# Decoder layer on one core: expert numbers worked out and loaded by TensorE during its warming products, row places later, query halves cleared by GpSimd

## The chip, the cores and the metric

The kernel runs on one core of a Trainium2 chip. The metric is the device time in microseconds (us) of one execution; the median of three runs is given. The engines are TensorE (PE in the profile, its weight loads PEld, its sequencer PEldq or PEq), VectorE (DVE), ScalarE (ACT), GpSimd (POOL) and SyncE (SP), whose queue issues the DMAs.

## The reference

The input x has 4 batches of 256 tokens with 256 features. Three blocks follow one another, each a residual with a layer norm behind it: causal self-attention with 16 heads of 16 features; an expert block in which the token's id chooses one of four experts; and a routed feed-forward block in which the token's own logits choose one of four larger experts.

```python
x = _layernorm(x + _L0_attn_ref(x, q_proj, k_proj, v_proj, o_proj))
x = _layernorm(x + _L0_xattn_ref(x, itok, ctx, ctx, ctx))
x = _layernorm(x + _L0_ffn_ref(x, Wr, br, Wg, Wu, Wd))
...
expert_ids = jnp.minimum(tid // tokens_per_expert, E - 1)      # second block
...
top_w, top_idx = jax.lax.top_k(probs, 1)                       # third block
```

## The kernel before, in words

The program is written out by hand for each engine; an engine works through its own list in order, and semaphores tie the lists together. Products are made in float16 with each float32 operand split in a high part (ScalarE) and a low part (VectorE), so that a product becomes three matmuls (`three`, line 1281).

**First stage.** The tokens are eight tiles of 128, two to a batch. `qkv(tt)` (lines 1297 to 1316) projects a tile: six matmuls of 512 columns for query and key, six of 256 for the value. ScalarE copies the high parts out (`proj_hi`, lines 566 to 582), VectorE the low parts (`proj_lo`, line 928, its instructions on line 935), TensorE transposes them (`stack_T`, lines 1318 to 1329), and VectorE and ScalarE copy the transposes into QT and KT (`stacks`, lines 942 and 945; `q_odds`, line 593). Then `scores(b, g)` (lines 1331 to 1366) makes the scores of four heads for the row maxima, which VectorE takes (`maxima`, lines 956 and 961), and `scores_T(b, g)` (lines 1368 to 1389) makes the transposed scores for the exponentials. The maxima of batch 0 go by four small DMAs (line 385) into a row of QT before `scores_T(0, 0)` may start. In QT the rows of a head's other half must be zero; those of QT[0] are cleared by VectorE (lines 920 and 921, semaphore `const_z`), those of QT[1] and QT[2] by GpSimd (lines 468 to 471, `const_q2`).

**Sorting.** Six of the eight tiles are sorted by the expert of the second block. VectorE makes one-hot rows from the ids (lines 898 to 904); TensorE counts them with two small matmuls (`count`, line 1274, lines 1278 and 1279); VectorE copies the counts out (`counts`, lines 818 and 819), sums them (`running`, line 812), and works out which expert each of the nine sorted tiles belongs to (`slot_tiles`, lines 801 to 808, the last instruction writes `tile_i` and raises `tile_rdy`). `slots` (lines 824 to 832) works out the row of every token (`pos_i`, semaphore `pos_rdy`), which GpSimd needs for the scatter of the first block's rows. `pick` (lines 906 and 907) is a table for the two tiles that aren't sorted. TensorE later reads the nine expert numbers into registers (`expert_numbers`, lines 1461 to 1463, four of them ahead of `qkv(2 * TB)`, five behind `stack_T(3)`), since the second block addresses its weights by them.

**Start of TensorE.** Behind the two count matmuls stand thirty products whose result nobody reads, `keep_warm(WARM_START, before)` (line 1442, the matmul on line 1291), then `qkv(0)`.

**Order of the queues around the change.** VectorE: one-hot rows, pick, low parts of x for batch 0 (line 911), low parts of the projection weights (line 916), counts, clearing of QT[0], low parts for batch 1, expert numbers, row places, then `proj_lo(0)`. GpSimd: constants and masks (lines 425 to 464), clearing of QT[2] and QT[1], then the fill row (lines 473 and 474), for which SP waits with two large DMAs that fill the scratch for sorted rows. SP: inputs, those two fills, the maxima's rows, then the chunks of the feed-forward weights (line 374), the first of which waits for `x_lo` of all four batches.

## Time and profile before

| | us |
|---|---|
| median of 3 runs | 292.88 |
| lowest and highest run | 290.88, 294.34 |
| profiled execution, its own time | 293.57 |
| span of that execution in the profile | 291.8 |
| TensorE busy, share of the span | 234.3, 80% |
| VectorE busy | 191.7, 66% |
| ScalarE busy | 135.3, 46% |
| GpSimd busy | 66.1, 23% |

The profile covers the one profiled execution; its instructions start at 0 and end at 291.8 us, so 1.8 us of that execution's time lie outside the span. Averages over the span say little here, since the change touches only the first 45 us of it. A timeline row is one or several like instructions of an engine in a row, with its idle time before them and what ended it; "issue" means that nothing the profile shows was waited for. The chain that ended last is followed back from the last instruction and printed in order of time.

### The profile page before, as it was taken

How to read it: one execution, taken by the hardware profiler on the slowest of the kernel's cores; microseconds unless marked ns; L12 is line 12 of the kernel's file. 1: busy time of each engine (PE TensorE's matmuls, PEld its weight loads, DVE VectorE, ACT ScalarE, POOL GpSimd, SP SyncE). 2: the span in 40 equal slices, each digit the busy share in tenths (PEclk: the TensorE clock that was granted, in tenths of full speed). 3: DMA queues.
4: the chain of work that ended last, by engine and by line, in shares of the span. 5: the costliest groups of instructions: out<-in, count | busy, mean ns of one | idle time of the engine just before them, and what ended most of it. 6: DMA issues, size and time to landing. Idle time of an engine off the chain costs nothing.

```text
span 291.8 us, 7077 instructions
## 1 busy us (share of the span) xinstructions
PE 234.3 (80%) x2714; PEld 189.1 (65%) x2730; DVE 191.7 (66%) x425; ACT 135.3 (46%) x229; POOL 66.1 (23%) x128
## 2 busy tenths in 40 slices
PE   4568678988899897599997346898778999999970
PEld 4356355665676664367796222598768999999960
DVE  4887648786699685569988452789535555556550
ACT  4536355766694885256555151488131333333300
POOL 8500000100020444212122556000113212222222
PEclk9999779999999999789999558999999999999996
DMA  6999244142024444602409412340000000000000
GB/s 189 340 315 318 74 144 152 67 147 72 3 85 135 109 115 177 163 2 72 147 20 403 161 59 81 94 111 2 0 20 20 4 13 20 21 20 20 7 5 15
DMA packets 17424, 28.63 MB, mean 98 GB/s; under 512 B 2733, under 2 KB 12974, under 8 KB 17392
## 3 DMA queue, kind: packets, MB, share of 16 engines
q1 hardware_dynamic: 16048, 25.28, 27.5%
q0 software_dynamic: 1344, 2.90, 2.8%
q8 instruction: 23, 0.38, 0.6%
q14 instruction: 9, 0.07, 0.1%
HBM read 19.43 MB, written 9.50 MB: 99 GB/s over the span
## 4 chain that ended last, share of the span: by engine, by line
PE 56%; DVE 21%; issue 9%; ACT 5%; POOL 4%; DMA 3%; SPq 1%; POOLq 0%; DVEq 0%; ACTq 0%
PE ps L1285 9%; PE ps L1678 7%; PE ps L1679 7%; PE ps L1680 7%; PE ps L1695 3%; PE ps L1697 3%; PE ps L1696 3%; DVE wf_lo L795 3%; PE ps L1362 3%; POOL sorted L519 2%; DVE arena L961 2%; PE ps L1614 2%; DMA ring<-wqkvT 2%; PE ps L1358 2%; ACT wf_hi L559 1%
## 5 line engine op out<-in xcount | busy, mean ns | idle before, releaser
L1678 PE MATMUL ps<-arena,wf_hi 128*128 128x128 f16 x352 | 60.2, 219 | 0.3 <-DVE arena L1197 0.3
L1679 PE MATMUL ps<-arena,wf_hi 128*128 128x128 f16 x352 | 60.3, 218 | 0.0
L1680 PE MATMUL ps<-arena,wf_lo 128*128 128x128 f16 x352 | 60.2, 217 | 0.0
L1679 PEld LDWEIGHTS ps<-arena,wf_hi 128*128 x352 | 34.3, 98 | 0.2
L1678 PEld LDWEIGHTS ps<-arena,wf_hi 128*128 x352 | 33.7, 96 | 0.9 <-issue 0.8
L1680 PEld LDWEIGHTS ps<-arena,wf_lo 128*128 x352 | 33.9, 96 | 0.0
L1695 PE MATMUL ps<-wf_hi,arena 128*128 x88 | 24.0, 273 | 5.9 <-DVE arena L1222 3.4
L795 DVE SCALAR_TENSOR_TENSOR wf_lo<-ring,wf_hi 128x1024 f16<-128x1024 f32 x17 | 20.6, 1219 | 11.0 <-ACT wf_hi L559 5.9
L751 ACT ACTIVATE arena<-ps 128x512 f32<-128x512 f32 x22 | 13.1, 594 | 29.7 <-PE ps L1680 29.7
L1697 PE MATMUL ps<-wf_hi,arena 128*128 x88 | 24.0, 273 | 0.0
L1696 PE MATMUL ps<-wf_lo,arena 128*128 x88 | 24.0, 273 | 0.0
L1285 PE MATMUL ps<-xT_hi,arena 128*128 (+1 forms) x88 | 21.5, 309 | 1.7 <-DVE arena L1137 1.1
L1206 DVE SCALAR_TENSOR_TENSOR arena<-ps,arena 128x512 f32<-128x512 f32 x22 | 15.2, 691 | 10.3 <-PE ps L1680 9.5
L758 ACT ACTIVATE arena<-arena 128x512 f16<-128x512 f32 x22 | 13.8, 629 | 16.6 <-DVE arena L1206 16.6
L1285 PE MATMUL ps<-arena,xT_hi 128*128 128x512 f16 (+1 forms) x64 | 16.5, 348 | 6.3 <-DVE xT_lo L911 2.6
L1213 DVE TENSOR_TENSOR arena<-arena 128x512 f16<-128x512 f32 x22 | 15.2, 691 | 8.8 <-ACT arena L758 8.8
L961 DVE TENSOR_REDUCE arena<-ps 128x4 f16<-128x1024 f32 x16 | 19.6, 1222 | 0.2
L536 POOL TENSOR_SCALAR veps<-mv 128x1 f32<-128x1 f32 x11 | 2.5, 226 | 71.1 <-DVE mv L1228 71.1
L559 ACT ACTIVATE wf_hi<-ring 128x1024 f16<-128x1024 f32 x17 | 17.7, 1054 | 0.1
L610 ACT ACTIVATE arena<-ps 128x1024 f32<-128x1024 f32 x16 | 16.6, 1036 | 1.1 <-PE ps L1385 0.7
L956 DVE TENSOR_REDUCE arena<-ps 128x4 f16<-128x512 f32 x16 | 11.0, 690 | 8.3 <-PE ps L1362 8.1
L1385 PE MATMUL ps<-arena 128*128 128x128 f16 x144 | 12.7, 227 | 3.3 <-issue 2.8
(223 smaller groups left out, 562.8 us busy)
## 6 DMA issues: line engine op xcount, KB each, us to landing
ring<-Wf SPq DMA_DIRECT2D x17, 512.0 KB, 3.7
sorted<-fill SPq DMA_DIRECT2D x1, 4515.0 KB, 20.8
arena<-Wf SPq DMA_DIRECT2D x7, 512.0 KB, 8.1
arena<-sorted SPq DMA_DIRECT2D x20, 129.0 KB, 2.3
sorted<-fill SPq DMA_DIRECT2D x1, 1161.0 KB, 6.3
ring<-xT SPq DMA_DIRECT2D x4, 256.0 KB, 5.1
X<-x_tok SPq DMA_DIRECT2D x1, 1024.0 KB, 7.8
ring<-ctxT SPq DMA_DIRECT2D x2, 512.0 KB, 3.6
```

Source lines behind the costliest of these rows:

```text
L559: a.activation(chunk_dst(ORDER[n], True), src, ACT.Copy, scale=W_SCALE).then_inc(c_hi, 1)
L610: a.activation(Pf[n % 2][:, 1:3], ps[:, 4:6, :], ACT.Exp, scale=DK ** -0.5).then_inc(exped, 1)
L795: v.scalar_tensor_tensor(out=chunk_dst(ORDER[n], False), in0=staged(n)[0], scalar=W_SCALE, in1=chunk_dst(ORDER[n], True), op0=ALU.mult, op ...
L961: v.tensor_reduce(dst[:, 1], ps[:, 1:3, :].rearrange("p c (a k) -> p a c k", a=G), AX.XY, ALU.max, negate=True).then_inc(maxed, 1)
L1206: v.scalar_tensor_tensor(out=hh[:, half * 512:(half + 1) * 512], in0=ps[:, 2 * half + 1, :], scalar=inv, in1=sg[:, half * 512:(half + 1) * ...
L1285: last = t.matmul(dst, xs(k), ws(k), start=(k == 0 and m == 0), stop=(k == nk - 1 and m == 2))
L1678: t.matmul(dst, hi, a_hi[p][:, k], start=k == 0, stop=False)
L1679: t.matmul(dst, hi, a_lo[p][:, k], start=False, stop=False)
L1680: last = t.matmul(dst, lo, a_hi[p][:, k], start=False, stop=k == NK - 1)
L1695: t.matmul(ps[:, 7, 0:D], hs[:, c], hi, start=c == 0, stop=False)
L1696: t.matmul(ps[:, 7, 0:D], hs[:, c], lo, start=False, stop=False)
L1697: last = t.matmul(ps[:, 7, 0:D], ls[:, c], hi, start=False, stop=c == NF - 1)
```

## The change

Five edits, all in the first stage:

1. VectorE works out the expert numbers (`counts`, `running`, `slot_tiles`) directly behind the one-hot rows, ahead of the low parts of x and of the weights.
2. VectorE makes `pick` and the row places (`slots`) later, behind `stacks(3)` and ahead of the low parts of batch 3 (`x_low(3)`) and of `maxima(1, 0)`.
3. The two clears of QT[0] go from VectorE to GpSimd, ahead of those of QT[2] and QT[1]; GpSimd waits for `const_z` between them.
4. TensorE makes 15 warming products in place of 30, waits for `tile_rdy`, and then loads the nine expert numbers, each followed by three more warming products (WARM_START // 10), 42 in all. The loads at the two later places are gone.
5. TensorE waits for `const_z` ahead of `scores(0, 0)`.

```diff
--- before.py
+++ after.py
@@ -465,6 +465,9 @@
                             base=0, pattern=[[0, G], [1, P]], channel_multiplier=-1).then_inc(const_m, 1)
 
             pool.wait_ge(const_m, 2)
+            link(g.memset(QT[0][SLOT:P, 0::2, :].bitcast(F32), 0.0))
+            g.memset(QT[0][0:SLOT, 1::2, :].bitcast(F32), 0.0).then_inc(const_z, 1)
+            pool.wait_ge(const_z, 1)
             link(g.memset(QT[2][SLOT:P, 0::2, :].bitcast(F32), 0.0))
             g.memset(QT[2][0:SLOT, 1::2, :].bitcast(F32), 0.0).then_inc(const_q2, 1)
             link(g.memset(QT[1][SLOT:P, 0::2, :].bitcast(F32), 0.0))
@@ -903,8 +906,11 @@
             link(ins)
             v.tensor_tensor(oh[:, 0:NA, :].rearrange("p i e -> p e i"), ge[:, 0:E, 0:NA], ge[:, 1:E + 1, 0:NA],
                             ALU.subtract).then_inc(oh_rdy, 1)
-            link(v.tensor_tensor(pick[:, :, :], ge[:, 0:E, NA:NT], ge[:, 1:E + 1, NA:NT], ALU.subtract))
-            v.tensor_scalar(pick[:, :, :], pick[:, :, :], 1 / W_SCALE, None, ALU.mult).then_inc(pick_rdy, 1)
+            counts()
+            dve.wait_ge(cnt_sb, 1)
+            running()
+            slot_tiles(0, NA)
+
             def x_low(b):
                 dve.wait_ge(x_hi, b + 1)
                 t = slice(b * S, (b + 1) * S)
@@ -915,15 +921,7 @@
                 dve.wait_ge(w_hi, k + 1)
                 v.scalar_tensor_tensor(out=wqkv_lo[:, k], in0=wqkv_st[:, k], scalar=W_SCALE, in1=wqkv_hi[:, k],
                                        op0=ALU.mult, op1=ALU.subtract).then_inc(w_lo, 1)
-            counts()
-
-            v.memset(QT[0][SLOT:P, 0::2, :].bitcast(F32), 0.0)
-            v.memset(QT[0][0:SLOT, 1::2, :].bitcast(F32), 0.0).then_inc(const_z, 1)
             x_low(1)
-            dve.wait_ge(cnt_sb, 1)
-            running()
-            slot_tiles(0, NA)
-            slots()
 
             def proj_lo(tt):
                 j = tt % 2
@@ -1029,6 +1027,9 @@
             stacks(2)
             proj_lo(2 * TB)
             stacks(3)
+            link(v.tensor_tensor(pick[:, :, :], ge[:, 0:E, NA:NT], ge[:, 1:E + 1, NA:NT], ALU.subtract))
+            v.tensor_scalar(pick[:, :, :], pick[:, :, :], 1 / W_SCALE, None, ALU.mult).then_inc(pick_rdy, 1)
+            slots()
             x_low(3)
             maxima(1, 0)
             dve.wait_ge(w_hi, NK + 1)
@@ -1439,7 +1440,12 @@
                                  lambda k: wo_hi[:, k], lambda k: wo_lo[:, k], NK)
                     last.then_inc(wo_rdy, 1)
 
-            keep_warm(WARM_START, before[:, :])
+            keep_warm(WARM_START // 2, before[:, :])
+            pe.wait_ge(tile_rdy, 1)
+            experts = []
+            for k in range(NSA):
+                experts.append(pe.value_load(tile_i[0:1, 0, k:k + 1], min_val=0, max_val=E - 1))
+                keep_warm(WARM_START // 10, before[:, :])
             pe.wait_ge(x_lo, 1)
             pe.wait_ge(w_lo, NK)
             qkv(0)
@@ -1448,6 +1454,7 @@
             stack_T(0)
             stack_T(1)
             pe.wait_ge(const_m, 1)
+            pe.wait_ge(const_z, 1)
             scores(0, 0)
             pe.wait_ge(x_lo, 2)
             qkv(2)
@@ -1456,19 +1463,10 @@
             scores(0, 2)
             stack_T(2)
             scores(0, 3)
-            experts = []
-
-            def expert_numbers(n):
-                for k in range(len(experts), n):
-                    experts.append(pe.value_load(tile_i[0:1, 0, k:k + 1], min_val=0, max_val=E - 1))
-
-            pe.wait_ge(tile_rdy, 1)
-            expert_numbers(4)
             pe.wait_ge(x_lo, 3)
             pe.wait_ge(maxed, 2 * NG - 1)
             qkv(2 * TB)
             stack_T(3)
-            expert_numbers(NSA)
             for step in range(STEPS):
                 b, g = divmod(step, NG)
                 if step == 0:
@@ -1545,7 +1543,6 @@
                                        identF[:, :])
                 last.then_inc(bhT, 1)
 
-            expert_numbers(NSA)
             for s in range(NS + LOGIT_LAG):
                 if s < NS:
                     k = sorted_of(s)
```

TensorE at the start, before: the warming products (L1291) and the first matmuls of `qkv(0)` (L1285).

```order
L1291 MATMUL ps<-before,ones 128x128 x30
L1285 MATMUL ps<-arena,xT_hi 128x512 [waits w_lo,x_lo]
L1285 MATMUL ps<-arena,xT_hi 128x512
L1285 MATMUL ps<-arena,xT_lo 128x512
L1285 MATMUL ps<-arena,xT_hi 128x512 x2
```

TensorE at the start, changed kernel, where one load is a TENSOR_LOAD with two more sequencer instructions (ISA) behind it:

```order
L1292 MATMUL ps<-before,ones 128x128 x15
L1447 TENSOR_LOAD tile_i [waits tile_rdy]
L1447 ISA x2
L1292 MATMUL ps<-before,ones 128x128 x3
L1447 TENSOR_LOAD tile_i
L1447 ISA x2
L1292 MATMUL ps<-before,ones 128x128 x3
L1447 TENSOR_LOAD tile_i
L1447 ISA x2
L1292 MATMUL ps<-before,ones 128x128 x3
L1447 TENSOR_LOAD tile_i
```

The pattern of one load and three products comes nine times, and the matmuls of `qkv(0)` stand behind the last. 

TensorE at the end of `scores(0, 3)` (L1358 and L1362), before, up to `qkv(2 * TB)`:

```order
L1358 MATMUL ps<-maskS,identB 128x512
L1362 MATMUL ps<-arena 128x128 x4
L1463 TENSOR_LOAD tile_i [waits tile_rdy]
L1463 ISA x2
L1463 TENSOR_LOAD tile_i
L1463 ISA x2
L1463 TENSOR_LOAD tile_i
L1463 ISA x2
L1463 TENSOR_LOAD tile_i
L1463 ISA x2
L1285 MATMUL ps<-arena,xT_hi 128x512 [waits maxed,x_lo]
L1285 MATMUL ps<-arena,xT_hi 128x512
```

The same place in the changed kernel, where line numbers are one higher:

```order
L1359 MATMUL ps<-maskS,identB 128x512
L1363 MATMUL ps<-arena 128x128 x4
L1286 MATMUL ps<-arena,xT_hi 128x512 [waits maxed,x_lo]
L1286 MATMUL ps<-arena,xT_hi 128x512
L1286 MATMUL ps<-arena,xT_lo 128x512
```

Nothing stands between the two any more; the five loads behind `stack_T(3)` are gone in the same way.

VectorE behind the one-hot rows, before (L911 and L916 are the low parts of x and of the weights):

```order
L904 TENSOR_TENSOR oh<-ge 128x4x6 [waits link_v]
L906 TENSOR_TENSOR pick<-ge 128x8
L907 TENSOR_SCALAR pick<-pick 128x8 [waits link_v]
L911 TENSOR_TENSOR xT_lo<-ring,xT_hi 128x2x256 [waits x_hi]
L916 SCALAR_TENSOR_TENSOR arena<-ring,arena 128x768 [waits w_hi] x2
L818 COPY cum<-ps 128x24 [waits cnt_rdy]
L819 COPY cnt<-ps 128x4x6
L920 MEMSET arena 64x8x128
L921 MEMSET arena 64x8x128
L911 TENSOR_TENSOR xT_lo<-ring,xT_hi 128x2x256 [waits x_hi]
L812 SCALAR_TENSOR_TENSOR run<-reset,cnt 128x44 [waits cnt_sb]
L801 TENSOR_TENSOR over<-run,steps 128x32 [waits link_v]
```

VectorE at the same place in the changed kernel:

```order
L907 TENSOR_TENSOR oh<-ge 128x4x6 [waits link_v]
L821 COPY cum<-ps 128x24 [waits cnt_rdy]
L822 COPY cnt<-ps 128x4x6
L815 SCALAR_TENSOR_TENSOR run<-reset,cnt 128x44 [waits cnt_sb]
L804 TENSOR_TENSOR over<-run,steps 128x32 [waits link_v]
L806 TENSOR_REDUCE nt_e<-over 128x4 [waits link_v]
L807 SCALAR_TENSOR_TENSOR end_e<-reset,nt_e 128x4 [waits link_v]
L808 TENSOR_TENSOR tile_ge<-tiles,end_e 128x33 [waits link_v]
L810 TENSOR_REDUCE tile_e<-tile_ge 128x11 [waits link_v]
L811 CAST tile_i<-tile_e 128x11 [waits link_v]
L917 TENSOR_TENSOR xT_lo<-ring,xT_hi 128x2x256 [waits x_hi]
L922 SCALAR_TENSOR_TENSOR arena<-ring,arena 128x768 [waits w_hi] x2
```

The nine instructions from the counts to `tile_i` moved ahead of the low parts, and the two clears are gone. VectorE behind `stacks(3)`, before:

```order
L942 COPY arena<-ps 128x8x128 [waits kT_rdy]
L945 COPY arena<-ps 64x8x128 [waits qT_rdy]
L911 TENSOR_TENSOR xT_lo<-ring,xT_hi 128x2x256 [waits x_hi]
L956 TENSOR_REDUCE arena<-ps 128x4 [waits s_rdy]
L961 TENSOR_REDUCE arena<-ps 128x4 [waits s_rdy]
```

VectorE behind `stacks(3)` in the changed kernel:

```order
L940 COPY arena<-ps 128x8x128 [waits kT_rdy]
L943 COPY arena<-ps 64x8x128 [waits qT_rdy]
L1030 TENSOR_TENSOR pick<-ge 128x8
L1031 TENSOR_SCALAR pick<-pick 128x8 [waits link_v]
L827 TENSOR_TENSOR base_e<-end_e,nt_e 128x4
L828 TENSOR_TENSOR run<-run,cnt 128x4x6 [waits link_v]
L829 SCALAR_TENSOR_TENSOR run<-base_e,run 128x4x6 [waits link_v]
L831 TENSOR_TENSOR where<-cum,run 128x24 [waits link_v]
L833 TENSOR_TENSOR where<-where,oh 128x24 [waits link_v]
L834 TENSOR_REDUCE pos<-where 128x6 [waits link_v]
L835 CAST pos_i<-pos 128x6 [waits link_v]
L917 TENSOR_TENSOR xT_lo<-ring,xT_hi 128x2x256 [waits x_hi]
```

Nine instructions for `pick` and `slots` now stand between the copies of `stacks(3)` and the low parts of batch 3, with the maxima of batch 1 behind those.

## Rows read from the trace of the kernel before

**Rows 1.** Chain that ended last, 0 to 60 us: start, duration, what.

```profile
16.16 0.69 DVE arena L942
...
30.52 0.50 issue
31.02 2.73 PE ps L1285 x6
...
36.24 0.60 DVE arena L945
...
42.00 1.23 DVE arena L961
```

**Rows 2.** TensorE timeline: start, duration, instruction, idle before it and releaser.

```profile
3.65 3.36 PE L1291 MATMUL ps<-before,ones 128*128 128x128 f16 x30
9.05 0.59 PE L1285 MATMUL ps<-arena,xT_hi 128*128 128x512 f16 x2 [2.03 <-DVE arena L916]
...
15.51 0.62 PE L1323 MATMUL ps<-identH,arena 128*128 128x128 f16 x8 [2.40 <-DVE arena L935]
...
19.11 0.61 PE L1362 MATMUL ps<-arena 128*128 128x128 f16 x8 [1.65 <-DVE arena L945]
...
31.02 1.01 PE L1285 MATMUL ps<-arena,xT_hi 128*128 128x512 f16 x2 [2.60 <-DVE xT_lo L911]
...
38.47 1.06 PE L1385 MATMUL ps<-arena 128*128 128x128 f16 x8 [2.79 <-issue]
```

**Rows 3.** Line 1463, sequencer of TensorE: count, minimum/median/maximum ns, first and last start.

```profile
L1463 PEldq TENSOR_LOAD <-tile_i x9: 294/303/978, 27.6 to 37.1; - x9
```

**Rows 4.** The same loads between 27 and 31 us only.

```profile
L1463 PEldq TENSOR_LOAD <-tile_i x4: 294/306/978, 27.6 to 30.3; - x4
```

**Rows 5.** VectorE timeline, 0 to 60 us.

```profile
4.84 1.08 DVE L911 TENSOR_TENSOR xT_lo<-ring,xT_hi 128x512 f16<-128x512 f32 x1 [0.74 <-ACT xT_hi L563]
...
8.91 0.17 DVE L819 COPY cnt<-ps 128x24 f32<-128x24 f32 x1
...
10.51 0.91 DVE L921 MEMSET arena<- 64x1024 f32 x1 [0.25 <-issue]
11.35 0.62 DVE L911 TENSOR_TENSOR xT_lo<-ring,xT_hi 128x512 f16<-128x512 f32 x1
11.89 0.23 DVE L812 TENSOR_TENSOR_SCAN run<-reset,cnt 128x44 f32<-128x44 f32 x1
...
13.26 0.17 DVE L808 CAST tile_i<-tile_e 128x11 int32<-128x11 f32 x1
...
14.62 0.17 DVE L832 CAST pos_i<-pos 128x6 int32<-128x6 f32 x1
...
41.27 0.69 DVE L956 TENSOR_REDUCE arena<-ps 128x4 f16<-128x512 f32 x1 [3.84 <-PE ps L1362]
```

**Rows 6.** GpSimd timeline, 0 to 60 us.

```profile
4.74 0.64 POOL L458 TENSOR_SCALAR_AFFINE_SELECT maskS<-maskS 128x512 bf16<-128x512 bf16 x1
...
6.86 0.95 POOL L468 MEMSET wf_hi<- 64x1024 f32 x1
```

**Rows 7.** Windows: PE, PEld, DVE, ACT, POOL busy, granted clock, DMA share, GB/s.

```profile
160.70:174.30 13.60, 5.04 (x20) 3.53 (x19) 6.58 (x37) 4.06 (x8) 8.00 (x10) 0.50 0.29 111
31.02:34.40 3.38, 3.38 (x11) 1.49 (x12) 1.34 (x3) 0.63 (x2) 0.00 (x0) 0.50 0.07 15
38.10:41.20 3.10, 2.73 (x20) 2.28 (x22) 0.00 (x0) 1.38 (x2) 0.00 (x0) 0.50 0.89 305
```

**Rows 8.** DMA issues by the SP queue, 0 to 60 us.

```profile
29.96 2.71 SPq L385 DMA_DIRECT2D arena<-arena  x4
37.46 12.78 SPq L374 DMA_DIRECT2D ring<-Wf  x5
```

**Rows 9.** Landing of the chunk DMAs of line 374, 36 to 60 us.

```profile
DMA to landing us min/median/max: 3.4/3.8/4.7
```

**Rows 10.** ScalarE timeline, first weight chunk.

```profile
46.63 1.06 ACT L559 ACTIVATE wf_hi<-ring 128x1024 f16<-128x1024 f32 x1
```

## Prediction

> **What bounds the kernel now.** I read the chain that ended last first, then the timelines of TensorE, VectorE and GpSimd for the first 45 us, then the sequencer's register loads, and last the windows with the granted clock. The reader is to see three things.
>
> First, TensorE is not short of work but of inputs. It stands idle for 2.03 us before `qkv(0)`, 2.40 us before the first transposes and 1.65 us before the first scores [rows 2], each time for VectorE. The chain runs over VectorE's copies from 16.16 us on [rows 1]. In the second gap VectorE is busy with two clears (0.91 us each, 0.25 us between), batch 1's low parts, the expert numbers (start of L812 at 11.89, end of L808 at 13.43) and the row places (until 14.79) [rows 5].
>
> Second, the nine expert numbers stand in TensorE's way twice. The loads are made by its sequencer, in order: four start between 27.6 and 30.3 us [rows 4], the last of nine at 37.1 us [rows 3]. The first took 0.978 us, the others about 0.30, but they follow each other at (30.3 - 27.6 - 0.68) / 3 = 0.67 us, since two further sequencer instructions belong to each. The low parts were there at 30.52 us, and `qkv(4)` started at 31.02 [rows 1]: 0.5 us is the loads'. VectorE's last copy ended at 36.84 us (36.24 + 0.60) [rows 1], and the transposed scores are first seen at 38.47 us, after 2.79 us of idleness put down to "issue" [rows 2]: some 1.3 us is the loads', the rest the first mask product, whose record is missing.
>
> Third, the clock. Behind the gaps of 2.60 and 2.79 us the granted clock is 0.50, the 1.2 GHz level: from 31.02 to 34.40 and from 38.10 to 41.20 us [rows 7]. Eight products of 128 columns take 1.06 us at 38.47 against 0.61 at 19.11 [rows 2]. Half of these 6.5 us is lost: 1.7 and 1.55 us.
>
> **The change, part by part.** All times are of the profiled execution.
>
> *Expert numbers first.* The count products are issued just ahead of 3.65 us [rows 2], so the counts can be copied at about 3.95 us. Two copies take 0.3 us (one is 0.17 [rows 5]) and the chain to `tile_i` 1.54 us (11.89 to 13.43): 5.8 us at the earliest. That chain ran with GpSimd nearly idle. Now it stands beside GpSimd's masks and clears (L458 from 4.74, L468 from 6.86 to 7.81 us [rows 6]), and beside them the subtraction on line 911 took 1.08 us in place of 0.62 [rows 5, 6]. If two of the chain's instructions are held by the masks, and its last waits for the end of L468, it ends at 8.0. I take 7.0, with 5.8 and 8.0 as ends.
>
> The Trainium skill ("SBUF — State Buffer", section "Who interferes with whom") says that VectorE and GpSimd share one port pair as an exclusive lock, which VectorE wants with two SBUF inputs against a reading GpSimd instruction, or in a two-port mode. By that rule the chain goes to the late end, 8.0 us, and the sum below becomes 1.0 us larger; were there no lock, 1.2 us smaller. The 1.08 us row agrees with the rule.
>
> *Loads at the start.* TensorE's sequencer waits there for `tile_rdy`. Queued behind it are the products between the loads and all of `qkv(0)`. The first load costs 0.98 + 0.37 = 1.35 us, eight more 0.67 each: 6.7 us, so that `qkv(0)` starts at 7.0 + 6.7 + 0.2 = 13.9 us instead of 9.05: +4.85. Nothing hides this: VectorE's work behind the chain is pushed back by 7.0 - 4.84 = 2.2 us at most [rows 5], so the low parts are there by 9.05 + 2.2 = 11.2 us. The 27 products between the loads are issued ahead of their running and cost the sequencer next to nothing; the upper end, if it waited for each three (3 x 0.112 us, from 3.36 / 30 [rows 2]), is 3.0 us more. Below, a first load without the 0.68 us of surplus gives 0.7 less.
>
> *Clock at `qkv(0)`.* Before, 30 unbroken products ran at the 1.2 GHz level (0.112 us apart), and `qkv(0)` met the 2.4 GHz level: two products of 512 columns in 0.59 us, against 1.01 at 31.02 [rows 2]. Now 15 products end near 5.3 us, a pause follows, then three at a time (0.34 us) in every 0.67. Each rise I see comes behind unbroken products, as those of 31.02 to 34.40 us; from 160.7 to 174.3 us, with products in 5.04 of 13.6 us, the clock stayed at 0.50 [rows 7]. So I let `qkv(0)` run at the low level and rise after some 3.3 us, as it did behind 31.02: +1.65. Ends: nothing, and +3.9 if `qkv(1)` is slow too.
>
> *What VectorE gives back.* Both projections took 4.05 us (9.05 to 13.10: 15.51 less 2.40); they now end at 13.9 + 4.05 + 1.65 = 19.6. VectorE has no clears, numbers or places left to do. The query and key part of `qkv(1)` (two thirds of its columns) is done at 18.95. At `qkv(4)` that part ended at 33.75 (31.02 + 2.73) and VectorE's two copies began at 36.84 - 1.2 = 35.65 [rows 1]: 1.9 us for the copies of ScalarE and the low parts. So `stacks(0)` starts at 20.85 instead of 16.16 [rows 1]: +4.7. So of 6.5 us, 1.8 comes back.
>
> *Loads gone at 28 us.* The gap before `qkv(4)` shrinks from 2.60 to 2.1 us, the 0.5 us is gained (+4.2), and I take the clock to stay at 1.00: the query and key part takes 1.35 in place of 2.73 us [rows 1]. VectorE's last copy ends at 36.84 + 4.2 - 1.35 = 39.7. Ends: all 1.35 lost if the clock falls.
>
> *Loads gone at 35 to 37 us.* The transposed scores follow the copy by 0.25 us, at 39.95 instead of about 38.1: +1.85. Their low stretch of 3.1 us is gone, 1.55 back: TensorE is +0.3 at 41.2 us.
>
> *`pick` and `slots` late.* Nine instructions, 1.4 us for `slots` (13.43 to 14.79 [rows 5]) and 0.35 for `pick` (an estimate, two more like them), from 39.7 to 41.5 us, then `x_low(3)` 0.62 (L911 [rows 5]): `maxima(1, 0)` starts at 42.15 instead of 41.27 [rows 5]: +0.9. The 3.84 us in which VectorE was idle there [rows 5] hid them before; now they outlast the scores. The second maximum was on the chain at 42.00 [rows 1] and starts at 42.75: +0.75, which the chain carries on. `pos_rdy` and `pick_rdy` are wanted by the scatters and the dense tiles, tens of us later.
>
> *The rest.* GpSimd's clears of QT[0] end at 8.8 us, long before the scores. They push the fill row, and so the fill DMAs, 2.0 us later. These were done at 31 us (DMA share 0.07 from 31.02 on [rows 7]), now at 33; the four DMAs of the maxima (issued 29.96 to 32.67 [rows 8]) now start at 34.6 and are in by 39. The first weight chunks wait for `x_low(3)`: 42.2 instead of 37.46 [rows 8], landing 3.8 us later [rows 9], at 46.0; ScalarE wants the first at 46.63 [rows 10], now 47.4. Hidden, by 1.4 us.
>
> **Sum.** +4.85 + 1.65 - 1.8 - 0.5 - 1.35 - 1.0 (loads at 37 us) - 1.55 + 0.5 (VectorE over TensorE) = +0.8 us. The profiled execution took 293.57, so 294.4; it stood 0.69 over the median of 292.88, so the forecast for the median is 293.7 us. A change within 1% is about what a measurement of this kernel can't tell from none.
>
> **The rivals.**
> - *A: loads cheap.* If the loads ran beside the warming products or at 0.3 us, `qkv(0)` would start at about 9.5, the copy of line 945 end at 36.84 + 0.45 - 2.3 (VectorE's clears and places) - 0.5 - 1.35 = 33.1, and `maxima(1, 0)` start at 35.6: 5.6 us less, 287.3. For it: the gaps at 13 to 15 us are real. Against: 0.67 us apart [rows 4] while little else ran.
> - *B: the clock is up at once.* 1.65 us less than forecast: 292.1. For it: the 15 products in front. Against: the stretch 160.7 to 174.3.
> - *C, slower: the low level lasts.* The broken products keep the clock at 0.50 until the scores: 3.9 instead of 1.65 us for both projections and 0.8 us more for the last sixteen transposes, 296.7 us. It decides if the clock is still 0.50 when `stack_T(1)` runs, near 21 us. For it: no rise in the trace comes behind broken products. Against: `qkv(0)` and `qkv(1)` are unbroken for over 5 us.
> - *D: the change doesn't do what it says*, in that the loads' 6.7 us don't leave the path but move to where TensorE has nothing else. This is the forecast itself.
>
> **How the numbers follow.** Forecast 0.52, C 0.22, A 0.13, B 0.13. Low end of the forecast's terms: -1.2 (chain) - 0.7 (first load) gives 291.8, with B 290.2. High end: +1.0 (chain) and a fall of the clock at `qkv(4)` +1.35 gives 296.1; C with the late chain 297.7. Range 290.2 to 297.2. Faster by over 1% (under 289.95): A and a little of B, 0.15. Slower by over 1% (over 295.8): most of C and a tail of the forecast, 0.20. Within 1%: 0.65.
>
> **What would show it.** Right: nine loads from 7 to 13.5 us, `qkv(0)` starting at 13 to 14.5 us at clock 0.50, no idle time on TensorE between `qkv(1)` and `stack_T(0)`, first scores near 23.5 us, `qkv(4)` behind the low parts within 0.1 us at clock 1.00, `maxima(1, 0)` at 42 behind x's low parts, and from there on all rows shifted alike. Wrong: `qkv(0)` before 11 us (A), a clock of 1.00 at its start (B) or of 0.50 at 21 us (C), a wait for the maxima's rows before the transposed scores, or a clock that falls elsewhere after 110 us.

## The result, and the profile after

The changed kernel took 296.86 us, median of four runs (295.34 to 299.03), against 292.76 for the kernel before beside it (290.88 to 294.34): ratio 1.0167, interval 1.0124 to 1.0211. A ratio leaves out disturbed (slow) executions, so it need not match the two medians beside it. The kernel is slower; the forecast was 293.7 us and no change worth speaking of. The time lies inside the stated range, but the kernel did change, by more than 1%.

| | before | after |
|---|---|---|
| median of the runs | 292.76 us | 296.86 us |
| profiled execution, its span | 293.57, 291.8 us | 296.75, 294.6 us |
| mean granted clock | 0.939 | 0.933 |

TensorE's timeline of the changed kernel, where it answers to [rows 2]:

```profile
3.65 1.76 PE L1292 MATMUL ps<-before,ones 128*128 128x128 f16 x15
6.99 0.50 PE L1292 MATMUL ps<-before,ones 128*128 128x128 f16 x3 [1.58 <-DVE tile_i L811]
...
12.36 0.50 PE L1292 MATMUL ps<-before,ones 128*128 128x128 f16 x3 [0.20 <-issue]
12.65 1.06 PE L1286 MATMUL ps<-arena,xT_hi 128*128 128x512 f16 x2
...
16.30 0.59 PE L1286 MATMUL ps<-arena,xT_hi 128*128 128x512 f16 x2
...
18.25 0.61 PE L1324 MATMUL ps<-identH,arena 128*128 128x128 f16 x8
...
22.52 0.61 PE L1363 MATMUL ps<-arena 128*128 128x128 f16 x8 [1.73 <-DVE arena L943]
...
33.98 0.60 PE L1286 MATMUL ps<-arena,xT_hi 128*128 128x512 f16 x2 [2.14 <-DVE xT_lo L917]
...
39.12 0.61 PE L1386 MATMUL ps<-arena 128*128 128x128 f16 x8 [2.13 <-DVE arena L943]
```

`qkv(0)` starts at 12.65 us in place of 9.05. Its products run at the 1.2 GHz level (two of 512 columns in 1.06 us), those of `qkv(1)` at 16.30 at 2.4 GHz (0.59). The first scores come at 22.52 us, 3.4 us late. But the transposed scores, at 39.12, are only 0.65 us behind the 38.47 of [rows 2], and eight of their products take 0.61 us where they took 1.06.

The nine loads by line, which answer to [rows 3, 4]:

```profile
L1447 PEldq TENSOR_LOAD <-tile_i x9: 294/304/493, 6.1 to 11.7; - x9
```

They again follow each other at (11.7 - 6.1 - 0.2) / 8 = 0.67 us. VectorE's timeline, against [rows 5]:

```profile
3.84 0.18 DVE L821 COPY cum<-ps 128x24 f32<-128x24 f32 x1 [0.39 <-PE ps L1280]
...
4.14 0.25 DVE L815 TENSOR_TENSOR_SCAN run<-reset,cnt 128x44 f32<-128x44 f32 x1
...
4.87 0.50 DVE L807 TENSOR_TENSOR_SCAN end_e<-reset,nt_e 128x4 f32<-128x4 f32 x1
...
5.86 0.17 DVE L811 CAST tile_i<-tile_e 128x11 int32<-128x11 f32 x1
5.94 0.79 DVE L917 TENSOR_TENSOR xT_lo<-ring,xT_hi 128x512 f16<-128x512 f32 x1
...
37.87 0.67 DVE L943 COPY arena<-ps 64x1024 f16<-64x1024 f16 x1
38.47 0.15 DVE L1030 TENSOR_TENSOR pick<-ge 128x8 f32<-128x8 f32 x1
...
40.10 0.69 DVE L917 TENSOR_TENSOR xT_lo<-ring,xT_hi 128x512 f16<-128x512 f32 x1
40.70 0.69 DVE L954 TENSOR_REDUCE arena<-ps 128x4 f16<-128x512 f32 x1
41.31 1.23 DVE L959 TENSOR_REDUCE arena<-ps 128x4 f16<-128x1024 f32 x1
```

The numbers were there at 6.03 us. The second maximum stands at 41.31 against 42.00 on the chain before [rows 1]: in these two executions the changed kernel is 0.69 us *ahead* there, and stays so up to 118 us (118.16 and 117.48 us for the same instruction of VectorE). What it loses, it loses later, where TensorE's clock is low. The windows of the changed kernel:

```profile
12.70:16.00 3.30, 3.30 (x12) 1.47 (x10) 0.00 (x0) 0.55 (x2) 1.15 (x6) 1.00 0.39 129
31.00:34.40 3.40, 1.26 (x12) 0.75 (x12) 3.19 (x6) 0.62 (x1) 0.00 (x0) 1.00 0.66 182
38.10:41.20 3.10, 2.08 (x28) 1.85 (x30) 2.86 (x12) 2.19 (x3) 0.00 (x0) 1.00 0.00 0
118.60:128.60 10.00, 7.88 (x36) 5.72 (x37) 3.85 (x10) 2.80 (x8) 0.04 (x1) 0.50 0.27 76
163.00:179.80 16.80, 8.35 (x26) 4.26 (x27) 6.86 (x38) 5.31 (x8) 11.05 (x14) 0.50 0.20 74
183.40:186.70 3.30, 3.30 (x9) 1.36 (x10) 2.16 (x2) 0.17 (x1) 0.00 (x0) 0.50 0.30 83
207.30:210.60 3.30, 3.30 (x18) 2.30 (x17) 0.21 (x1) 0.00 (x0) 0.00 (x0) 0.50 0.00 0
```

and of the kernel before, for the same stretches of its work:

```profile
119.80:126.50 6.70, 5.40 (x24) 3.76 (x25) 3.22 (x9) 2.31 (x6) 0.00 (x0) 0.50 0.36 100
160.80:177.70 16.90, 8.27 (x28) 4.67 (x27) 8.17 (x45) 5.70 (x9) 9.98 (x13) 0.50 0.25 95
183.40:186.70 3.30, 2.20 (x14) 0.90 (x12) 1.87 (x3) 1.32 (x3) 0.00 (x0) 1.00 0.36 91
207.30:210.60 3.30, 3.30 (x51) 3.16 (x49) 1.16 (x4) 0.49 (x1) 0.44 (x2) 1.00 0.00 0
```

A warning for the reading of the clock column: the window at 12.70 says 1.00, and the products in it take 1.06 us for two of 512 columns, the time of the low level. In all these profiles the column reads 1.00 up to the first fall, whatever the products take; there the durations have to be read (here they turn short between 16.06 and 16.19 us).

Two explanations of 4 us were open: something in the first stage that this pair of profiles hides, or low stretches in the last two blocks that the change brings about.

### The profile page after: what moved, and what is told of

Same layout as the page of the kernel before. It is cut to its first block, busy times and chain, and to the rows that moved or that the text cites. A ratio compares the mean times of both kernels' runs of the same rounds, so it can differ in the third digit from the quotient of the medians.

```text
span 294.6 us, 7101 instructions
## 1 busy us (share of the span) xinstructions
PE 240.1 (81%) x2726; PEld 190.9 (65%) x2742; DVE 189.6 (64%) x423; ACT 135.4 (46%) x229; POOL 68.7 (23%) x130
## 4 chain that ended last, share of the span: by engine, by line
PE 59%; DVE 20%; issue 9%; ACT 5%; POOL 3%; DMA 2%; POOLq 0%; DVEq 0%; ACTq 0%
PE ps L1286 11%; PE ps L1675 7%; PE ps L1676 7%; PE ps L1677 7%; PE ps L1692 4%; PE ps L1693 3%; PE ps L1694 3%; PE ps L1292 3%; PE ps L1363 2%; DVE arena L959 2%; DVE wf_lo L798 2%; PE ps L1611 2%; POOL sorted L522 2%; ACT wf_hi L562 1%; DVE arena L954 1%
## 5 line engine op out<-in xcount | busy, mean ns | idle before, releaser
L1692 PE MATMUL ps<-wf_hi,arena 128*128 x88 | 24.7, 281 | 5.9 <-DVE arena L1223 3.4
L1693 PE MATMUL ps<-wf_lo,arena 128*128 x88 | 24.8, 282 | 0.0
L1694 PE MATMUL ps<-wf_hi,arena 128*128 x88 | 24.8, 281 | 0.0
L1286 PE MATMUL ps<-xT_hi,arena 128*128 (+1 forms) x88 | 22.5, 318 | 2.0 <-DVE arena L1138 1.4
L543 POOL DMA_INDIRECT out<-arena,out_i x11 | 12.0, 1091 | 13.9 <-DVE arena L1235 13.9
L933 DVE SCALAR_TENSOR_TENSOR arena<-ps,arena 128x256 f16<-128x256 f32 x16 | 6.0, 419 | 13.6 <-ACT arena L582 13.6
```

What stands on the lines that cost most here:

```text
L1286: last = t.matmul(dst, xs(k), ws(k), start=(k == 0 and m == 0), stop=(k == nk - 1 and m == 2))
L1692: t.matmul(ps[:, 7, 0:D], hs[:, c], hi, start=c == 0, stop=False)
L1693: t.matmul(ps[:, 7, 0:D], hs[:, c], lo, start=False, stop=False)
L1694: last = t.matmul(ps[:, 7, 0:D], ls[:, c], hi, start=False, stop=c == NF - 1)
```

## The experiments

**The moment at which the products begin.** The first idea was that the low stretches behind 118 us depend on when TensorE's products begin. `late_warm` and `later_warm` are the kernel before with a wait in front of the warming products and nothing else moved:

```diff
+            pe.wait_ge(const_m, 1)          # late_warm
             keep_warm(WARM_START, before[:, :])

+            pe.wait_ge(const_m, 2)          # later_warm
-            keep_warm(WARM_START, before[:, :])
+            keep_warm(2 * WARM_START // 3, before[:, :])
```

`warm_whole` is the changed kernel with all 30 products ahead of the loads; `vector_only` has VectorE's and GpSimd's part of the change, with TensorE's products and loads as before.

```diff
-            keep_warm(WARM_START // 2, before[:, :])      # warm_whole, from the changed kernel
+            keep_warm(WARM_START, before[:, :])
```

> The kernel before, with one wait more: the thirty warming products start behind GpSimd's first mask (about 5.4 us) instead of at 3.65 us, and end by about 8.9 us, so that the first projection still starts near 9.05 us at the 2.4 GHz level. Nothing else changes. Theory 1 (when the clock first rises decides at which later pauses of TensorE it falls): the first 100 us are as before within 0.3 us, the rise comes about 1.8 us later than at 7.1 us, and the falls after 110 us lie elsewhere and last longer or shorter; the time moves by 1.5 us or more, either way, all of it behind 110 us. Theory 2 (the loss lies in the late fill, the late row places or the moved expert numbers): same as before within 0.5 us, about 292.8.

> The kernel before, with the warming products (20 instead of 30) starting behind GpSimd's second mask at about 6.85 us. The first projection starts near 9.05 us still at the low level and loses about 0.6 us until the rise near 10.3 us. Theory 1: the moments at which the clock may change lie again nearly where they lay before, so the later falls are those of before, and the time is 0.3 to 1.0 us over before, 293.1 to 293.8; the first kernel of this call moves more than this one though its start is disturbed less. Theory 2: 0.6 us over before for the same reason, and the first kernel at nothing.

> The changed kernel with 30 instead of 15 products ahead of the loads, so that they run unbroken from 3.65 to 7.0 us, while the sequencer already makes the first load. Theory 1: the clock rises near 7.1 us as before; it may fall again during the three-product groups and rise during the first projection, but its changes stay where the kernel before has them, so the falls after 110 us are those of before, and with the first stage 0.6 us or more ahead the time is 291 to 293.5 us. Theory 2: nothing changes against the changed kernel, 296 to 297 us, since the loads end at 12.4 us all the same.

> The changed kernel with TensorE's part taken back: thirty unbroken warming products at 3.65 us, the loads at their two old places, four and five. VectorE's and GpSimd's parts are those of the change. Theory 1: the first scores come near 17 us instead of 19.1, the second projection group and the transposed scores 1.5 to 2 us earlier, less what the row places take back on VectorE (1.8 us), the clock rises at 7.1 us as before: 291 to 293 us. Theory 2 (the late fill or the row places cost the time): the 4 us stay, 296 to 297.

| | median (range) of its runs, us | before on the same chip | ratio, interval |
|---|---|---|---|
| late_warm | 294.02 (291.15 to 295.91) | 294.14 | 0.9993, 0.9958 to 1.0029 |
| later_warm | 294.53 (290.20 to 296.24) | 294.14 | 0.9897, 0.9826 to 0.9968 |
| warm_whole | 298.02 (295.22 to 302.08) | 294.14 | 1.0110, 1.0070 to 1.0150 |
| vector_only | 297.11 (294.77 to 300.71) | 294.14 | 1.0112, 1.0068 to 1.0157 |

`later_warm` has the lower ratio and the higher median, so it says nothing firm. The products of `late_warm` begin 1.8 us later (5.43 for 3.65 us) and its ratio has no room for the 1.5 us that theory 1 wanted, so the idea falls. `warm_whole` has twice the products in front and still first rises to the high level at 16.1 us, as the changed kernel does. `vector_only` is slow without any of TensorE's part. So VectorE's and GpSimd's part alone brings 3.0 us in the whole kernel, most of the loss. And the runs of the one kernel before went from 291.05 to 297.27 us here: a single profile is one draw from a spread wider than the effect.

**Where the loss is: the program cut.** To get the spread down I cut the program behind attention. The cut kernels leave out the second and third blocks (the expert block and the routed feed-forward block), and write X1, the rows that the attention block left, instead. All kernels named `stage_` are cut so.

```diff
             for m in range(n - RING, n):            # SP, then `return` on every engine
+                sp.wait_ge(*staged(m)[1:])
+            sp.wait_ge(res1, NT)
+            sp.wait_ge(x1_rdy, NA)
+            sp.dma_start(out.rearrange("(n p) d -> p n d", p=P), X1[:, :, 0:D]).then_inc(in_late[0], 16)
```

> The kernel before, cut off behind the attention stage (about 118 us): no second and third block; the first six token tiles after the first norm and the last two before it are written out as the result. It is the yardstick for the next two: about 118 us and one transfer of 1 MB, 124 to 128 us. Its executions spread with the clock's changes in the first 45 us, by up to 3 us.

> The changed kernel with the same cut. Theory A (the 4 us are lost in the first stage, in most executions, and the profiled ones happen to be good for the changed kernel and bad for the one before): its median is 3 to 4 us over that of the kernel before with the same cut. Theory B (the first stage is as the profiles show it, 0.7 us ahead, and the loss lies behind the attention, where the clock falls more often): its median is 0.7 us under to 0.5 us over.

> VectorE's and GpSimd's parts of the change alone, with the loads at their old places and 30 warming products, with the same cut. Theory A: 3 us over the kernel before with this cut, as its full version was. Theory B: within 1 us of it.

`stage_before` took 123.12 us (122.70 to 124.75), `stage_after` 125.81 (123.49 to 126.03), `stage_vector` 125.36 (123.82 to 126.94), six executions each on one chip. So by the medians 2.7 us are lost in the first stage, where the pair of full profiles had shown 0.69 us of gain: theory A, a little under its 3 to 4 us. That leaves 4.1 - 2.7 = 1.4 us of the whole kernels' loss that the cut kernels don't show. It may lie behind attention, where the changed kernel's profile has low stretches that the other lacks (183.40 and 207.30 us), or in the spread between sets of runs: the kernel before had medians of 292.49 to 294.19 us on the chips used here. Which of the two isn't shown.

The cut kernels below ran on four chips. The kernel before's medians beside them were 292.49 us (with `stage_before`), 293.84 (`stage_slots` to `clears`), 293.62 (`stage_loads` to `held`) and 294.19 (`stage_four` to `stage_held`), so a difference of under about 1 us between cut kernels of different sets isn't firm.

The rows where TensorE had waited, `stage_before` first:

```profile
9.12 1.01 PE L1297 MATMUL ps<-arena,xT_hi 128*128 128x512 f16 x2 [2.11 <-DVE arena L926]
...
19.19 0.61 PE L1374 MATMUL ps<-arena 128*128 128x128 f16 x8 [1.65 <-DVE arena L955]
31.13 0.59 PE L1297 MATMUL ps<-arena,xT_hi 128*128 128x512 f16 x2 [2.64 <-DVE xT_lo L921]
36.95 1.06 PE L1397 MATMUL ps<-arena 128*128 128x128 f16 x8 [2.81 <-issue]
43.07 0.62 PE L1335 MATMUL ps<-identH,arena 128*128 128x128 f16 x8 [0.32 <-DVE arena L966]
```

and `stage_after`:

```profile
22.12 1.06 PE L1375 MATMUL ps<-arena 128*128 128x128 f16 x8 [1.89 <-DVE arena L953]
35.07 0.72 PE L1298 MATMUL ps<-arena,xT_hi 128*128 128x512 f16 x2 [2.14 <-DVE xT_lo L927]
41.29 0.61 PE L1398 MATMUL ps<-arena 128*128 128x128 f16 x8 [1.52 <-ACT arena L605]
45.96 0.62 PE L1336 MATMUL ps<-identH,arena 128*128 128x128 f16 x8 [0.32 <-DVE arena L964]
```

with its two low windows:

```profile
21.80:25.10 3.30, 2.98 (x16) 1.94 (x18) 1.72 (x2) 0.00 (x0) 0.00 (x0) 0.50 1.10 235
35.50:38.80 3.30, 3.30 (x14) 1.75 (x13) 1.52 (x4) 1.08 (x2) 0.00 (x0) 0.50 0.05 8
```

Against [rows 2], this execution of the old order runs `qkv(4)` at the high level (0.59 for 1.01) and reaches the transposed scores at 36.95 in place of 38.47; this one of the new order has a low stretch from its first scores on and another inside `qkv(4)`, and reaches them at 41.29. A later row, the transposes behind the first maximum of batch 1, stands behind both places. The two full profiles, before first, have it at

```profile
44.48 0.62 PE L1323 MATMUL ps<-identH,arena 128*128 128x128 f16 x8 [0.32 <-DVE arena L956]
```

```profile
43.79 0.62 PE L1324 MATMUL ps<-identH,arena 128*128 128x128 f16 x8 [0.32 <-DVE arena L954]
```

The profile before was a slow draw in its first stage (44.48 for 43.07, 1.41 us), the profile after a quick one (43.79 for 45.96, 2.17 us): -0.69 + 1.41 + 2.17 = +2.89 us, which is how far apart the two cut profiles are.

**VectorE's edits one by one.** Three kernels, each `stage_before` with one of them:

```diff
+            link(v.tensor_tensor(pick...)); slots()     # shortened; stage_slots: only here, behind stacks(3)
             x_low(3)
             maxima(1, 0)

+            counts(); dve.wait_ge(cnt_sb, 1); running(); slot_tiles(0, NA)   # stage_numbers: only here
             x_low(0)

-            v.memset(QT[0]...)                          # stage_clears: by GpSimd behind const_m 2
```

`clears` is the third in the whole kernel.

> First stage alone, cut as stage_before was (second and third blocks left out), with one part of the change: pick and the row places moved behind stacks(3), in front of x_low(3) and maxima(1, 0). Theory L (the late row places are what costs): they stood at 13.41 to 14.85 us in front of proj_lo(0), and now hold maxima(1, 0) back by 1.6 us of VectorE's time, so the median is 1 to 1.6 us above stage_before's 123.1 (124.1 to 124.7). Theory F (it is when TensorE stands idle and then runs at the low level that costs, and the places are worth nothing by themselves): proj_lo(0) is 1.4 us earlier, scores(0, 0) too, and what is given back at the start pays for what is lost at 38 us: 122.3 to 123.6.

> First stage alone, same cut, with one part of the change: counts, running counts and tile numbers on VectorE ahead of x_low(0); row places, pick, the clears of QT[0] and TensorE's loads stay where they were. Theory L: x_low(0) and so qkv(0) start about 1.1 us late, but VectorE has the same time less to do before proj_lo(0), so nothing is left of it: 122.6 to 123.8. Theory F: qkv(0) starts later after the warming products, TensorE is idle between 7 and 10 us for longer, and qkv(0) falls to the low level in most executions, as in stage_vector's profile (9.75 to 13.16 us): 124.3 to 125.6, low level within 9.7 to 14 us in the profile.

> First stage alone, same cut, with one part of the change: QT[0] cleared by GpSimd instead of VectorE. VectorE has 2.0 us less between 9.4 and 11.4 us. Both theories: proj_lo(0) starts 1.5 to 2.1 us earlier, scores(0, 0) as well, unless x_low(1) waits for its rows. Theory L: the gain reaches the end, 121.2 to 122.4. Theory F: the gain is taken back where TensorE waits for scores, x_low(2) and maxima anyway: 122.3 to 123.5.

> The whole kernel with that one part (QT[0] cleared by GpSimd, all else as before). Theory L: 1 to 2 us faster than before on the same chip, ratio 0.993 to 0.997. Theory F: ratio 0.998 to 1.002, and the profile shows the start ahead by 1.5 us or more up to about 30 us and not behind it.

They took 123.38 us (122.73 to 125.84), 123.28 (123.02 to 124.67) and 123.50 (122.42 to 124.66): none differs from 123.12 by anything firm. `stage_numbers`' profile has the low level from 10.20 to 13.50 us, as theory F wanted, and took 123.09 us, so there it cost nothing. Both theories' larger figures fall: the late row places cost nothing alone and the moved clears give nothing alone. In `stage_slots`' profile the first maximum waits for its scores long after row places and `x_low(3)` are done:

```profile
36.77 0.17 DVE L842 CAST pos_i<-pos 128x6 int32<-128x6 f32 x1
36.85 0.68 DVE L919 TENSOR_TENSOR xT_lo<-ring,xT_hi 128x512 f16<-128x512 f32 x1
...
39.37 0.69 DVE L963 TENSOR_REDUCE arena<-ps 128x4 f16<-128x512 f32 x1 [1.83 <-PE ps L1374]
```

`clears`, the whole kernel, took 295.69 us (293.58 to 298.99) against 293.84, ratio 1.0085 (1.0038 to 1.0132). That is slower by more than its interval, which neither theory had, and the cut kernel shows only 0.4 us of it. I can't say from what. In its one profile, one of its longer executions (298.15 us), the clock is also low behind attention from 208 to 212 and from 222 to 225.5 us (windows of 0.57 and 0.51, where the kernel before has 1.00); that this is the rule is not shown.

**TensorE's part, a pair, and a short warming.** `stage_loads` adds to `stage_numbers` what the change does on TensorE; `stage_pair` has early numbers and late row places; `stage_half` is `stage_before` with 15 products.

```diff
-            keep_warm(WARM_START, before[:, :])           # stage_loads, from stage_numbers
+            keep_warm(WARM_START // 2, before[:, :])
+            pe.wait_ge(tile_rdy, 1)
+            experts = []
+            for k in range(NSA):
+                experts.append(pe.value_load(tile_i[0:1, 0, k:k + 1], min_val=0, max_val=E - 1))
+                keep_warm(WARM_START // 10, before[:, :])

-            keep_warm(WARM_START, before[:, :])           # stage_half, from stage_before
+            keep_warm(WARM_START // 2, before[:, :])
```

> First stage alone, same cut: stage_numbers plus TensorE's part of the change (15 products, then the nine loads with groups of three products, ahead of qkv(0)); row places, pick and the clears of QT[0] as before. Theory R (TensorE's part is what costs: broken products and loads keep the clock from rising before qkv(0), so qkv(0) and qkv(1) run at the low level, longer in some executions than in others): median 125.2 to 126.0, as stage_after's 125.8, the first rise in the profile at 14.5 us or later. Theory S (it needs clears and row places as well, since each part alone was worth nothing): 123.2 to 124.3.

> First stage alone, same cut: numbers early and row places late together, clears of QT[0] still on VectorE, TensorE as before; stage_vector without the moved clears. Theory R: the VectorE part costs by where the low level happens to lie, not by one of its edits, so 123.2 to 124.3 and a wide range. Theory S: early numbers and late row places together are stage_vector's loss, 124.8 to 125.6.

> First stage alone, same cut: the kernel before with 15 warming products in place of 30 and nothing else, so that TensorE stands idle from about 5.4 to 9.05 us. Theory R: the clock does not rise before qkv(0), which runs at the low level; rise at 12 us or later, median 124.5 to 126. Theory S: qkv(0) at the low level hides behind VectorE's row places and clears, which stand in front of proj_lo(0) here, so 123.0 to 123.8.

`stage_loads` took 125.99 us (124.13 to 126.41), 2.7 above `stage_numbers`, from which it differs on TensorE alone: theory R's size. `stage_half` took 123.97 (122.74 to 124.94), 0.85 above `stage_before` and between the two theories' ranges: three executions at 122.7 to 123.3, three at 124.6 to 124.9. Its `qkv(0)` started in time, at 9.18 us, and at the low level. There VectorE's clears and row places stand behind the projections and hide most of that: `stage_before`, whose `qkv(0)` also ran low in its profile (1.01), has its first scores at 19.19 us, against 19.11 for a `qkv(0)` at the high level [rows 2]. In `stage_loads` they don't hide it, since VectorE is done with them at 13.5 us and the transposes follow `qkv(1)` at once, at 17.76: the two projections take 5.11 us there for 4.05. So the low level is worth some 1 us of `stage_loads`' 2.7, by this one profile, and not all. `stage_pair` took 124.25 (121.40 to 125.58), inside R's range, three executions at 121.4 to 123.2 and three at 125.3 to 125.6.

**Place of the loads, or clock.** Two edits to `stage_loads` that tell these apart: four loads in front and five behind `stack_T(3)`; and all nine in front without the products between them.

```diff
-            for k in range(NSA):                 # stage_four; the other five behind stack_T(3)
+            for k in range(4):

-                keep_warm(WARM_START // 10, before[:, :])     # stage_no_groups
```

> First stage alone, same cut: stage_loads with only the first four loads (and their groups of products) ahead of qkv(0); the other five behind stack_T(3), where they were before. Theory P (the nine loads cost by where they stand: qkv(0) starts at 12.65 us in stage_loads' profile and at 9.05 in stage_numbers'): four loads end by 9.0 us, so qkv(0) starts at 9.1 to 9.4, and the median falls from stage_loads' 126.0 to 123.3 to 124.4. Theory C (it is the clock, which the broken products keep from rising before qkv(0)): the products are as broken as before, qkv(0) at the low level, 125.0 to 126.0.

> First stage alone, same cut: stage_loads without the groups of three products between the loads, so that TensorE multiplies nothing from 5.4 to about 12.6 us. Theory P: the groups hide behind the loads, which come 0.67 us apart with or without them; qkv(0) at 12.4 to 12.7, median 125.5 to 126.3, as stage_loads' 126.0. Theory C: the clock rises later still, and the median is above 126.5.

`stage_four` took 123.76 us (121.70 to 125.21), `stage_no_groups` 125.54 (123.82 to 125.84): both medians are theory P's. In `stage_four` the products were as broken as before and `qkv(0)` ran low, but it started at 9.26 us and not at 12.65, the first scores came at 19.61 and not at 22.14, and the median is 2.2 us lower. Three of its executions lie at 124.8 to 125.2 all the same, so its median stands between two groups. `stage_no_groups` is not above 126.5, as C wanted, with the first rise at 18.2 us against 15.1 in `stage_loads`. That doesn't show that the clock is free: its profile lacks the low stretch of `stage_loads` at 21.80 to 25.10 us, and the low level lasted about as long in both. Its row:

```profile
12.26 1.01 PE L1297 MATMUL ps<-arena,xT_hi 128*128 128x512 f16 x2 [6.86 <-DVE xT_lo L926]
```

against `stage_numbers`:

```profile
9.05 0.59 PE L1297 MATMUL ps<-arena,xT_hi 128*128 128x512 f16 x2 [2.12 <-DVE arena L931]
```

The start of `qkv(0)` moves by the loads' own time, with products between them or without (0.39 us less). Over all cut kernels: with nine loads in front 13 of 18 executions took over 125 us, and the quickest of each kernel 123.49 to 124.13; with none in front and at most one of VectorE's edits (`stage_before`, `stage_slots`, `stage_numbers`, `stage_clears`, `stage_half`), 2 of 30, and the quickest 122.42 to 123.02. So the medians' 2.7 us hold two things: the quick executions are some 1 us slower, and far more of the executions are long ones.

**What the two low stretches were worth.** `held` is the whole kernel before with products between its loads, in the places where TensorE had stood idle ahead of `qkv(4)` and of the transposed scores; `stage_held` is the same, cut.

```diff
+HOLD = 2
             for k in range(len(experts), n):
                 experts.append(pe.value_load(tile_i[0:1, 0, k:k + 1], min_val=0, max_val=E - 1))
+                for _ in range(HOLD if bank is not None else 0):
+                    t.matmul(ps[:, bank, :], identB[:, :], maskS[:, :, :].rearrange("p a k -> p (a k)"),
+                             start=True, stop=True)
-            expert_numbers(4)
+            expert_numbers(4, bank=7)
             stack_T(3)
+            pe.wait_ge(kT_done, 3)
-            expert_numbers(NSA)
+            expert_numbers(NSA, bank=3)
```

> The whole kernel before, all its parts, with two products of 128x512 behind each of the nine loads of expert numbers, in bank 7 for the first four (at 28 us) and bank 3 for the others (at 35 us). Theory R and every theory in which idle TensorE ahead of qkv(2 * TB) and of the transposed scores brings the low level at 31.0 to 34.4 and 37.8 to 41.2 us: neither stretch is at the low level in the profile, and the time is 0.5 to 2.5 us below before's on the same chip (ratio 0.991 to 0.998). If the stretches at the low level only come later: ratio 0.999 to 1.003.

> First stage alone, same cut: held, cut. If the stretches at the low level around 31 and 38 us are what an ordinary execution of the kernel before has, taking them away gives 2 to 2.9 us: 120.2 to 121.2. If its profiled execution was one with more of them than most, less: 121.5 to 122.7 (whole kernel: held's median was 1.15 us below that of before).

`held` took 292.47 us (290.11 to 294.94) against 293.62, ratio 0.9935 (0.9896 to 0.9974). It is faster than the kernel before, and so than the changed one. `stage_held` took 122.09 (121.87 to 122.77), 1.0 below `stage_before` (on another chip), and its five executions lie closer together than those of any other cut kernel. Its windows:

```profile
10.10:13.40 3.30, 3.30 (x12) 1.64 (x11) 2.88 (x9) 1.47 (x3) 1.30 (x6) 0.50 1.07 353
28.00:31.40 3.40, 2.81 (x17) 0.92 (x15) 3.23 (x7) 0.45 (x1) 0.00 (x0) 1.00 0.94 243
31.40:34.80 3.40, 3.40 (x33) 2.29 (x31) 1.89 (x6) 1.63 (x4) 0.00 (x0) 1.00 0.09 18
34.80:38.20 3.40, 3.19 (x23) 1.32 (x22) 1.85 (x4) 1.80 (x3) 0.00 (x0) 1.00 0.15 24
```

From 28 to 38 us TensorE is busy in 9.4 of 10.2 us, and the level is high. Neither stretch of [rows 7] is there, and by the medians that is worth 1.0 us, not the 2.9 which the one profile put on them. The 1.0 is net: `qkv(4)` starts at 31.49 us behind the added products and at 31.13 in `stage_before`. One reason why it isn't more stands in the profiles of the five cut kernels with the loads at their old places and at most one of VectorE's edits: four have one low stretch between 30 and 42 us (`stage_half` and `stage_numbers` at `qkv(4)`, `stage_before` and `stage_slots` behind it), and only `stage_clears` has both, as [rows 7] do.

## Why the prediction was wrong

**Right:**
- *Loads at the start.* 13.9 us was forecast for `qkv(0)`, it was 12.65. The step of 0.67 us for a load held to the hundredth. The difference, 1.25 us, is the chain (ready at 6.03 us, 7.0 taken, 5.8 the early end) and the first load's surplus, 0.2 us and not 0.68.
- *The chain and the port.* The Trainium skill ("SBUF — State Buffer", section "Who interferes with whom") led to the late end, 8.0 us. The chain's seven instructions took from 4.14 to 6.03, 1.89 us against 1.54 before; one scan with two inputs took 0.50 us for 0.17 beside GpSimd's mask, which agrees with the rule. But what contention there was cost 0.35 us, far from the late end.
- *Clock at `qkv(0)`.* Low, and up at 16.1 us, some 3.4 us on. The two projections took 5.6 us (12.65 to 18.25) for 4.05: +1.55, with +1.65 forecast. But that the kernel before has the high level there was also one draw: `stage_before` and `held` start `qkv(0)` at the low level behind the same 30 products (1.01 us for two).
- *What VectorE gives back.* Transposes straight behind `qkv(1)` (18.25 us), `stacks(0)` at 19.58; first scores 3.4 us late, with a start 3.6 us late and 1.55 us lost to the clock: 1.7 given back, 1.8 forecast.
- *`pick` and `slots` late.* They occupied VectorE from 38.47 to 40.19 us, as long as I thought. I charged 0.75 us; it was nothing, since the first maximum at 40.70 came as its scores ended.
- *No wait for the maxima's rows, chunks hidden.* Neither shows in the trace.

**The step that failed** is the clock behind `qkv(1)`: "I take the clock to stay at 1.00" at `qkv(4)`, -1.35 us, with "their low stretch ... is gone", -1.55 us, and no term at all for a low stretch anywhere else in the changed kernel. In the profiled execution of the changed kernel it all came true (0.60 us at 33.98; 1.00 in the windows at 31.00 and 38.10), and the rows from 41 us on show even -0.69 us. But the terms took two stretches at the low level out of a single execution of the kernel before, as if they belonged to the kernel, and gave the changed kernel none. What the runs showed in its place:

- *In the kernel before.* `stage_before`'s profile has `qkv(4)` at the high level, so the 1.35 us weren't there to be gained, and is 1.5 us earlier at the transposed scores. With both stretches filled, `stage_held` is 1.0 us quicker, not 2.9.
- *In the changed kernel.* `stage_after` has a low stretch at 21.80 to 25.10 us and another inside `qkv(4)`, after an idle time of 2.14 us which the change had left there; so has `stage_loads`. From the first scores to `qkv(4)` it takes 12.95 us against 11.94 in `stage_before`, where the sum has -0.5, and from there to the transposed scores 6.22 against 5.82, where the sum has -2.35. The second low stretch did go: 4.67 us against 6.12 from the transposed scores to the transposes behind the first maximum, -1.45 for the -1.55 forecast.

With 1.0 in place of 2.9 my sum would be +0.8 + 1.9 = +2.7 us, just what the cut kernels measured, but that agreement is luck. The start was 1.25 us too late in it and the 0.75 for `pick` and `slots` was nothing; with those put right too it is +0.7, and the other 2 us are the changed kernel's own low stretches (2.17 us between its two profiles).

I had written the other end of the first term down ("all 1.35 lost if the clock falls"), but priced it as an accident of the changed kernel, with the kernel before fixed at its profile. The forecast's chances rested on it as well.

**The rivals.** A fell: the loads are not cheap, and `stage_no_groups` shows that they cost nearly the same with nothing beside them (`qkv(0)` at 12.26 us). B fell: two products took 1.06 us. Rival C (the low level lasts) came nearest in time, 296.7 us (with the late chain 297.7, above the 297.2 at which my range ended), but its condition, 0.50 near 21 us, did not hold in the changed kernel's profile; the clock rose, and in `stage_after` and `stage_loads` fell again at the first scores. D was right in what it says: the nine loads moved from where they were mostly hidden (0.5 us of the first four showed [rows 1, 4]) to where each delays `qkv(0)`.

**What stays open.** `stage_vector` (VectorE's and GpSimd's edits, no loads in front) took 125.36 us, with 3 of 6 executions over 125, and so had `stage_pair`. Each edit alone cost nothing. `stage_vector`'s profile shows the low level from 30.30 to 37.00 us, over `qkv(4)` and the transposes behind it:

```profile
9.80:13.10 3.30, 3.30 (x12) 1.66 (x11) 0.54 (x2) 1.46 (x3) 3.13 (x4) 0.50 0.83 271
30.30:37.00 6.70, 5.21 (x26) 3.17 (x27) 3.07 (x8) 1.47 (x3) 0.00 (x0) 0.50 0.66 167
```

That the combination more often meets this is my guess, argued from one profile and not shown. This very execution was the quickest of the six, 123.82 us at a mean granted clock of 0.946, and another took 126.94 at 0.948; so how long the clock is low doesn't settle the time; where it is low, or something else such as the arrival of the inputs, may have its share. No run separates these. Nor do the costs add: VectorE's part is worth 2.2 us alone, TensorE's part 2.7 with the numbers, and all together 2.7. How the excess of `clears` in the whole kernel arises, and where the 1.4 us are that the cut kernels don't show, is open too.

## What to carry to other kernels

A stretch at the low clock in one profile is one draw: before its removal goes into a sum, look at the spread of the runs, or profile a neutral variant, and give it a chance on both sides, in the kernel before as in the one after. Register loads on an engine's sequencer cost their spacing wherever something ready stands behind them; put them where the engine waits for others anyway, and fill the gaps between them with products there, as `held` does. When an effect drowns in the spread, cut the program behind the stage in question; here the range of the kernel before fell from 6 us (28 executions) to 2 (6 executions, and fewer executions alone narrow a range). What such a cut doesn't show may still lie behind it.

## What the runs showed of the hardware

The level of TensorE's clock differs between executions of one program. `stage_after` took 123.49 us at a mean granted clock of 0.995 and 126.03 at 0.959, with four others between in time. The Trainium skill ("TensorE: Matmul & The Clock Gate", section "What's actually happening") says that the number of slow products at the start varies from run to run of one kernel, and puts the penalty of that ramp at under 1% of a typical kernel's span. The first half agrees: `qkv(0)` starts low in `stage_before` and high in the profile before. The second speaks of the start alone. Here low stretches in the middle of the kernel came and went too, and the executions of `stage_after` lie 2% apart: with the change at issue worth 1 to 2%, this spread decided the sign that a pair of profiles showed.

The same idle time comes before either level. Behind 2.14 us of it `qkv(4)` ran at the high level in the changed kernel's profile (1.00 from 31.00 to 34.40 us and later) and fell to 0.50 half a microsecond in in `stage_after`'s.

The mean granted clock doesn't order the times: four executions of `stage_after` took 125.7 to 125.9 us, three of them at 0.983 or 0.984 and one at 0.958.

Three products between two register loads cost next to nothing (loads 0.67 us apart, 6.99 to 12.36 us, and `qkv(0)` at 12.65 against 12.26 without them). They bought nothing that the times show either: the first rise came at 15.1 us in `stage_loads` against 18.2 without them, for a median 0.45 us longer, which is within the spread.
